# Half-channel slots for a selective scan, with scan input in matmul memory and C products on GpSimd

## The reference

```python
x = layernorm(x)                       # per position, over 256 features
x_ssm, z = split(x @ in_proj_w.T)      # 2 x 512 channels
xc = silu(causal_conv4(x_ssm) + conv_b)
xp = xc @ x_proj_w.T                   # 1 + 16 + 16 rows: dt_r, B, C
dt = softplus(dt_r @ dt_proj_w.T + dt_proj_b)
h  = exp(dt * A_n) * h + dt * B_n * xc # for each of 16 states n, over 512 positions
y  = sum_n(h_n * C_n) + xc * D
out = (y * silu(z)) @ out_proj_w.T
x1 = x + layernorm(out);  x2 = layernorm(x1)   # x2 feeds the attention block
scores = sigmoid(x2 @ w_sel)
```

## Time and profile before

| | us |
|---|---|
| median of three runs | 4357.64 |
| the profiled execution | 4360.78 |
| its span | 4358.8 |
| VectorE busy | 3630.8 (83%) |
| TensorE busy | 3803.9 (87%) |
| GpSimd busy | 2849.6 (65%) |
| ScalarE busy | 2029.6 (47%) |

### The profile page before, as it was taken

One profiled execution on the slowest core, in us unless ns is written; L12 is line 12 of the kernel. 1 busy time (PEld: TensorE's weight loads), 2 busy tenths in 40 slices (PEclk: granted clock), 3 DMA queues, 4 the chain that ended last, 5 costly groups with the idle time before them and its releaser, 6 DMA issues. The chain is left out here.

```text
span 4358.8 us, 54031 instructions
## 1 busy us (share of the span) xinstructions
PE 3803.9 (87%) x15744; PEld 2541.1 (58%) x15744; DVE 3630.8 (83%) x4012; ACT 2029.6 (47%) x3761; POOL 2849.6 (65%) x2524
## 2 busy tenths in 40 slices
PE   6777867867765599999999999999999999999787
PEld 2233323323322377777777777777777777777676
DVE  5999999999998478877887887887888788778598
ACT  4544535535443244544444444444444444444433
POOL 2758668567594366766766766766766766766444
PEclk8877877877876799999999999999999999999898
DMA  1000000000000300100100100100100100000101
GB/s 39 0 10 15 24 5 19 24 5 19 15 5 20 131 13 12 41 14 10 41 14 10 41 14 10 41 14 10 41 14 10 41 14 10 20 14 15 31 29 44
DMA packets 48726, 97.83 MB, mean 22 GB/s; under 512 B 3570, under 2 KB 33138, under 8 KB 46228
## 3 DMA queue, kind: packets, MB, share of 16 engines
q1 hardware_dynamic: 47620, 92.94, 6.2%
q0 software_dynamic: 1040, 4.19, 0.2%
HBM read 80.34 MB, written 16.78 MB: 22 GB/s over the span
## 5 line engine op out<-in xcount | busy, mean ns | idle before, releaser
L702 DVE TENSOR_TENSOR_SCAN state<-dA,dBx 128x2048 f32<-128x2048 f32 x128 | 726.8, 5678 | 25.9 <-POOL y_part L289 21.3
L1234 ACT ACTIVATE prob<-ps_b,negmax 128x512 f32<-128x512 f32 x512 | 346.1, 687 | 652.3 <-DVE negmax L1353 652.3
L286 POOL TENSOR_TENSOR state<-state,c_copy 128x1024 f32<-128x1024 f32 x120 | 345.5, 2879 | 374.8 <-DVE state L702 374.8
L1347 DVE TENSOR_TENSOR vg<-ps_b,gates 128x1024 f32<-128x1024 f32 x256 | 313.5, 1224 | 253.1 <-PE ps_b L1072 241.1
L961 POOL TENSOR_TENSOR qk_full<-vg 128x512 f32<-128x512 f32 x256 | 329.0, 1285 | 253.3 <-DVE vg L1347 253.3
L549 ACT ACTIVATE dA<-dt,a_neg 128x511 f32<-128x511 f32 x512 | 326.9, 711 | 323.9 <-DVE state L702 323.7
L974 POOL TENSOR_TENSOR ogT_low<-prob,ogT_high 128x512 fp32r<-128x512 f32 x256 | 324.0, 1295 | 208.9 <-ACT ogT_high L1267 208.9
L372 PE MATMUL ps_a<-xp_high,ident_r 33*128 33x512 f32 x256 | 163.0, 637 | 332.6 <-DVE dBx L692 307.9
L1070 PE MATMUL ps_b<-ogT_high,wo_high 128*128 128x512 f32 x1024 | 413.2, 403 | 11.1 <-DVE ogT_low L1399 10.8
L1070 PE MATMUL ps_b<-wv_high,xT_high 128*128 128x512 f32 x1024 | 414.6, 405 | 0.0
L289 POOL TENSOR_TENSOR y_part<-y_part,state 128x1024 f32<-128x1024 f32 x120 | 403.4, 3362 | 9.4
(11 more groups left out here) (237 smaller groups left out, 9530.9 us busy)
## 6 DMA issues: line engine op xcount, KB each, us to landing
xT<-xT_scratch SPq DMA_DIRECT2D x65, 512.0 KB, 3.3
wv<-in_wv SPq DMA_DIRECT2D x8, 1024.0 KB, 4.9
wo<-in_wo SPq DMA_DIRECT2D x8, 1024.0 KB, 7.0
x_in<-in_x SPq DMA_DIRECT2D x8, 512.0 KB, 4.7
x_a<-in_x SPq DMA_DIRECT2D x8, 512.0 KB, 5.3
x_scratch<-x_a SPq DMA_DIRECT2D x8, 512.0 KB, 2.9
xT_scratch<-x2T SPq DMA_DIRECT2D x8, 512.0 KB, 2.6
scores_scratch<-sg SPq DMA_DIRECT2D x8, 512.0 KB, 3.5
```

The lines of the kernel that those rows point to most:

```text
L286: pool.tensor_tensor(state, state, c, ALU.mult).then_inc(hc_part_done, 1)
L702: dve.tensor_tensor_scan(h[n % 2][:, :, :].rearrange("p c s -> p (c s)"), dA[n % 2][:, :, :].rearrange("p c s -> p (c s)"), dBx[n % 2][:, ...
L1234: act.activation(prob[h][:, t, :], ps[:, score_bank(t) + h, :], ACT.Exp, bias=negmax[:, t, h:h + 1], accum_out=total[:, h, t:t + 1]).then_ ...
```

## The change

1. *Half-channel slots.* A turn has 32 slots instead of 16 steps: slots 0 to 15 run all states over the first two channel blocks, 16 to 31 over the other two. `dA` and `h` become rings of four half-size buffers.
2. *`dBx` in PSUM.* It has no SBUF buffer any more, but two PSUM banks, one buffer in all. So the B product of slot s+1 waits for the scan of slot s, and the scan of s+1 for the product. B's spread gets two banks.
3. *C products on GpSimd.* GpSimd multiplies the whole half state by C_n, in place (L371 of the new kernel); TensorE sums all blocks. VectorE's C product, GpSimd's accumulation, `y_part`, ScalarE's copy and TensorE's spread of C go. C's 16 rows go to DRAM once a turn, and come back spread over all partitions in four DMAs of four rows (1 MB each).
4. *One product a spread.* The high and low parts of `xp` lie in one tile of 97 rows (`xp_parts`), and `pick` adds both in one product.
5. *Norms.* Combining and refining move to GpSimd (`combine_pool`, `newton_pool`), with one operation more a norm; statistics and normalising stay on VectorE.
6. *Order.* z is projected at the start of its own turn (slots 0 to 3) instead of at the end of the turn before; step sizes come in halves; `sum_y` runs two slots late; skip and gate come in halves (slots 2 and 18); scores are made in slots 30 and 31 instead of steps 8 to 10.

Cut to its core:

```diff
+        HALF = CB // 2
+        SLOTS = 2 * NS
+        RING, GROUP = 4, 4
+        Y_BANK, DBX_BANK, B_BANK = 0, 2, 4
-        dA, dBx, h = ([sb(f"{name}{n}", [P, CB, S]) for n in range(2)] for name in ("dA", "dBx", "state"))
+        dA, h = ([sb(f"{name}{n}", [P, HALF, S]) for n in range(RING)] for name in ("dA", "state"))
+        c_rows = sb("c_rows", [P, NS, S])
...
+            def load_c(b, q, weighed=None):
+                at = slice(q * GROUP, (q + 1) * GROUP)
+                rows = d["c_rows"][bass.ds(b, 1), at].rearrange("b n s -> b (n s)").partition_broadcast(P)
+                if weighed is not None:
+                    sp.wait_ge(hc_done, weighed)
+                sp.dma_start(c_rows[:, at, :].rearrange("p n s -> p (n s)").unsqueeze(1), rows).then_inc(c_loaded[q], 16)
...
             def turn(i, par, has_tail, has_head):
+                b, c = i + 1, i - 1
                 if has_head:
                     sp.wait_ge(ln_x.out_done, i * TT + TT)
-                    load_x(i + 1)
+                    load_x(b)
                 if has_tail:
-                    tail(i - 1)
+                    load_c(i, 3, i * SLOTS)
+                    residual(c)
+                if has_head:
+                    store_c(b)
+                    for q in range(3):
+                        load_c(b, q, i * SLOTS + NS + GROUP * (q + 1))
+                if has_tail:
+                    store_x2T(c)
+                    store_scores(c)
...
+            def weigh(i, s):
+                n, state = s % NS, h[s % RING][:, :, :]
+                pool.wait_ge(scan_done, i * SLOTS + s + 1)
+                if s < NS and n % GROUP == 0:
+                    pool.wait_ge(c_loaded[n // GROUP], i * 16 + 16)
+                pool.tensor_tensor(state, state, c_rows[:, n, :].unsqueeze(1).to_broadcast([P, HALF, S]), ALU.mult).then_inc(hc_done, 1)
...
+            def spread_b(b, s, par, first=False):
+                row = 1 + s % NS
+                if s == 0:
+                    pe.wait_ge(xp_low_done, b + 1)
+                if not first:
+                    pe.wait_ge(dBx_done, b * SLOTS + s - 1)
+                pe.matmul(ps[:, B_BANK + s % 2, :], pick[:, row:row + 1].to_broadcast([XPP, P]), xp_parts[par][:, :],
+                          start=True, stop=True).then_inc(b_psum, 1)
...
+            def inputs(b, s, par, first=False):
+                f = s // NS
+                if s % NS == 0:
+                    dve.wait_ge(du_done, b * CH + f + 1)
+                if not first:
+                    dve.wait_ge(scan_done, b * SLOTS + s)
+                dve.wait_ge(b_psum, b * SLOTS + s + 1)
+                dve.tensor_tensor(ps[:, DBX_BANK:DBX_BANK + HALF, :], half(du[par], f),
+                                  ps[:, B_BANK + s % 2, :].unsqueeze(1).to_broadcast([P, HALF, S]), ALU.mult).then_inc(dBx_done, 1)
+            def scan(i, s, first):
+                dve.wait_ge(dA_done, (i * SLOTS + s + 1) * HALF)
+                dve.wait_ge(dBx_done, i * SLOTS + s + 1)
+                if not (first and s < RING):
+                    dve.wait_ge(y_psum, i * SLOTS + s - RING + 1)
+                dve.tensor_tensor_scan(h[s % RING][:, :, :].rearrange("p c s -> p (c s)"),
+                                       dA[s % RING][:, :, :].rearrange("p c s -> p (c s)"),
+                                       ps[:, DBX_BANK:DBX_BANK + HALF, :].rearrange("p c s -> p (c s)"),
+                                       0.0, ALU.mult, ALU.add).then_inc(scan_done, 1)
```

The new `turn` of TensorE, which fixes what stands between the sums:

```diff
+                for s in range(SLOTS):
+                    if s + 2 < SLOTS:
+                        spread_b(i, s + 2, par)
+                    elif has_head:
+                        spread_b(b, s + 2 - SLOTS, 1 - par)
+                    if s < CB:
+                        project_z(i, s, has_tail)
                     if has_head:
+                        if s == 6:
+                            turn_input(b)
+                        elif 11 <= s < 15:
+                            project_x(b, s - 11, has_tail)
+                        elif 15 <= s < 23:
+                            convolve(b, (s - 15) // 2, range(0, 2) if s % 2 == 1 else range(2, 4))
+                        elif s in (24, 25):
+                            project_xp(b, 1 - par, range(2 * (s - 24), 2 * (s - 23)))
+                        elif s in (27, 28):
+                            project_dt(b, 2 * s - 54)
+                            project_dt(b, 2 * s - 53)
                     if has_tail:
+                        if 7 <= s < 11:
+                            project_out(c, s - 7, b if has_head else None)
+                        elif s == 29:
+                            turn_x2(c, b if has_head else None)
+                        elif s in (30, 31):
+                            select(c, s - 30)
+                    if s >= 2:
+                        sum_y(i, s - 2, has_tail or s - 2 >= NS)
+                    elif has_tail:
+                        sum_y(c, SLOTS - 2 + s, True)
```

More of the change, by code:

```diff
@@ L252, in _ @@
                 sp.dma_start(t[:], d[n]).then_inc(consts_loaded, 16)
+            store_c(0)
+            for q in range(NS // GROUP):
+                load_c(0, q)
             turns(sp, turn)
-            tail(NB - 1)
+            residual(NB - 1)
+            store_x2T(NB - 1)
+            store_scores(NB - 1)
             sp.wait_ge(x1_stored, CREDIT + 16 * NB)
@@ L291, in turn @@
[L291 to L302 removed]
+                low = xp_parts[par][LOW_ROW:XPP, :]
@@ new lines, in project_out @@
+            def project_out(c, t, b=None):
+                bank, at = EVEN[t // 2], slice(t * P, (t + 1) * P)
+                if t == 0:
+                    pe.wait_ge(yz_done, c * CH + CH)
+                    pe.wait_ge(zs_done, (c + 2) * CB if b is not None else NB * CB)
+                    if b is not None:
+                        pe.wait_ge(xnT_done, b * KD + KD)
+                for k in range(CB):
+                    mm = pe.matmul(ps[:, bank, (t % 2) * D:(t % 2 + 1) * D], yz[:, k, at], w_out[:, k, :],
+                                   start=(k == 0), stop=(k == CB - 1))
+                if t % 2:
+                    mm.then_inc(mo_psum, 1)
@@ L781, in _ @@
             last = NB - 1
-            skip(last, last % 2)
+            skip(last, 1, last % 2, first=True)
             stats_m(last)
```

612 lines of the change are left out of this document (306 added, 306 removed).

## The result

The changed kernel takes 4069.4 us, the median of four runs (4064.8 to 4070.1), against 4358.9 for the kernel before on the same chip (4356.7 to 4361.2, four runs): a ratio of 0.9335 (95% interval 0.9322 to 0.9348), 289 us less. The forecast was 4100, with a range of 4040 to 4215. The profiled execution took 4069.7 us with a span of 4067.9 and a mean granted clock of 0.972.

What follows compares the result with a forecast made beforehand. VectorE was taken to pace the first stage's loop: steady turns 171.0 to 138 us, six saving 198, first 30, last 28, rest 0, so 4360.8 becomes 4105, and the median, 3 lower, 4100 rounded; range 4040 to 4215.

Steps and rivals of the forecast that it cites:

- The step that carried the sum: On VectorE, with one input in matmul memory the scan stops taking turns with GpSimd and takes 2.29 us.
- Rival C: The scan still takes turns with GpSimd though one input left SBUF: slot 4.75, turn 164, 4305 us; 8%.
- 32 slots: VectorE's half states in a turn, each scan 2.29, B product 1.21, hand-overs 0.16: 3.66 us, 117 in all.
- other VectorE work: Rest of VectorE's turn: three times statistics and normalising, the residual add, four skip products: 12.3 us.
- stalls: VectorE waiting for late TensorE sums or the next input's load: 8.5 us a turn (ends 0 and 17).
- Rival D's cheap hand-overs: On VectorE, hand-overs as cheap as independent starts: slot 3.36 us, with the forecast's stalls 4023 us; 4%.
- the rival of dearer operands: Operands in matmul memory cost more than their rows say: each 0.1 us on an operation 51 us, 4150; 2%.
- each stretch at the lower level adds 1.7: TensorE, some 4.5 us late after slot 31, falls 1.7 us further behind with each stretch at the lower clock.
- The inventory of 117 us a turn: TensorE's work at the full level: 32 slots 69 us, projections and the rest 48, total 117, 12 under VectorE.
- Rivals B and E: B: TensorE becomes the bound at today's clock, 4240 us, 15%; E: TensorE stays at the lower level, above 4800 us, 5%.
- The ends: First turn 126 us, 30 less; last 130, 28 less; before and behind the loop 0, within 8 us either way.
- rival D's "no stall": Less is lost in the loop's turns: no stall, 4035 us; 9%.

Runs made afterwards that it cites:

- e1: The changed kernel with dBx in one SBUF buffer instead of two PSUM banks, order and waits the same: 4356.7 us, ratio 1.0002.
- e8: The kernel before with GpSimd's C product and accumulation for states 1 to 15 cut to the first of 512 positions: 4150.0 us, ratio 0.9525.
- e11: e1 with GpSimd's C product cut to the first of 512 positions: 4073.1 us, ratio 0.9348.
- e12: e11 with two SBUF buffers for dBx, so the B product waits only for the scan before the last: 4023.2 us, ratio 0.9233.
- e6: The changed kernel with VectorE's statistics and normalising operations laid singly into the gaps before and behind a B product: 4084.2 us.
- e4: The changed kernel with B's spread product done twice (4067.5 us) or four times (4085.2 us) in each slot.
- e9: The changed kernel with each normalising group between scan and B product, and GpSimd's C product of that slot held until the group is through: 4051.1 us.

## Why the prediction was right, and where its sizes were off

The step that carried the sum was that the scan stops taking turns with GpSimd once one input leaves SBUF. It holds: 2284 ns on average for 2.29 forecast, and e1, e8 and e11 show it from three sides. Rival C is out. e1 is what it describes, and shows it priced too low: 4305 forecast, 4357 measured, though the slot is 4.59 and not 4.75, since the waits of the other work were not in its price. The terms of one steady turn, by the starts of the fourth turn's scans:

| term | forecast | measured |
|---|---|---|
| 32 slots | 117 (3.66) | 119.4 (3.73) |
| other VectorE work | 12.3 | 13.4 |
| stalls | 8.5 | 2.3 |
| turn | 138 | 135.1 |

- *The slot.* Scan and GpSimd product were right to 0.01. The B product takes 1.23, not 1.21, and the hand-overs 0.12 and 0.09, not twice 0.08: 0.07 a slot, 18 us over the 256. Rival D's cheap hand-overs did not come, and neither did the rival of dearer operands: into matmul memory the B product takes 1229 ns, into SBUF 1221 (e11). The Trainium skill, "VectorE: DVE Perf Modes", section "The DRAIN you can't avoid", finds that a semaphore behind each of eight copies adds nothing over one behind the last. e12 is another test: it keeps every semaphore, lets the B product wait for the scan before the last instead of the one just ahead, and gets 0.24 us a slot. So what costs here is the wait, and no run tests the page's own case.
- *The other work.* Normalising was put at 1.4 us a norm and costs 2.03 of slot time (slot 5: 5.76 against 3.73), 1.9 more a turn. This is where the mechanism was incomplete. I had looked at operations with two SBUF tensors only; this one reads one, and still takes turns. The first stage before could not show it: none of its 96 normalising operations (405 to 414 ns) lay beside a GpSimd operation. The last stage of the same trace did, in the one that normalises from SBUF beside GpSimd:

```profile
L112 DVE TENSOR_SCALAR fn<-f,ln_avgb,ln_rstdb x32: 401/1340/1471, 4138.3 to 4344.9; 128x256 f32<-128x256 f32 x32
```

  The Trainium skill states it: "SBUF — State Buffer", section "Who interferes with whom", says that `tensor_scalar` can enter a two-port mode and then contends with GpSimd like an operation with two SBUF inputs, and that the other side blocks for the whole instruction. The rows agree: up to 1412 ns in the changed kernel, 2425 in e6. The statistics go the other way: a group of 1.41 adds only 1.13 to its slot, since it overlaps the B product ahead and the scan behind it.
- *The stalls.* This term was mis-sized most: 8.5 us a turn forecast, 2.3 measured. The next input's load was to be 2 to 6 us late a turn; VectorE waited for it 0.5 us in the whole loop. TensorE was to be 4.5 late behind slot 31; what VectorE waited for in the loop was this (us in total, times, longest):

```profile
DVE state L790 <- PE ps_a L503: 7.9, 15, 1.3
DVE ps_a L781 <- DVE state L790: 4.1, 12, 0.5
DVE state L790 <- issue: 4.1, 2, 2.0
```

  Seven turns share 7.9 us of waits for TensorE, in 15 scans. Twelve of these are the scans of slots 20 and 21, the other three those of slots 1, 4 and 5; the forecast had them at 30 to 3. Most begin with TensorE's order: in slot 18 it waits for the skip product, which stands behind VectorE's longest slot (17, 8.56 us):

```profile
532.84 3.78 PE L503 MATMUL ps_a<-state,ident 128*128 128x512 f32 x4 [7.65 <-DVE yz L802]
...
536.76 2.29 DVE L790 TENSOR_TENSOR_SCAN state<-dA,ps_a 128x1024 f32<-128x1024 f32 x1 [0.42 <-PE ps_a L503]
...
541.61 2.29 DVE L790 TENSOR_TENSOR_SCAN state<-dA,ps_a 128x1024 f32<-128x1024 f32 x1 [1.20 <-PE ps_a L503]
```

  After that wait the four products take 3.78 us, as at the lower level; the granted clock from 530 to 540 us is 0.55, and 0.93 in the 10 us ahead:

```profile
520.00:530.00 10.00, 5.19 (x13) 2.00 (x11) 9.71 (x12) 1.33 (x2) 3.94 (x9) 0.93 0.15 52
530.00:540.00 10.00, 7.16 (x10) 3.23 (x11) 9.19 (x8) 7.81 (x12) 8.87 (x9) 0.55 0.00 0
```

  The two waits that follow cost VectorE 1.6 us (0.42 and 1.20). They fit the forecast's "each stretch at the lower level adds 1.7", since four products at the full level take 1.9 us less; no run separates the clock from the late start.
- *TensorE.* The inventory of 117 us a turn came out at 116.9, and the loop's granted clock at 0.95, where 0.9 or more was named for the forecast. The close match is partly luck: 117 was counted at the full level, and this turn had a granted clock of 0.94, so at the full level its work is somewhat less. e4 shows the room left. Rivals B and E are out.
- *GpSimd and the C rows.* GpSimd is busy 95.5 us a turn, 105 forecast. The C rows load in 5.5 us each (4 to 5 forecast); in the loop nothing on VectorE or GpSimd is put down to them:

```profile
c_rows<-c_scratch SPq DMA_DIRECT2D x32, 1024.0 KB, 5.5
```

- *The ends.* First turn 121.1 (126 forecast), last 125.9 (130), the piece behind the loop within 2 us of before, as taken. The start is 4 us shorter (56.9 against 61.1), within the 8 allowed for. The stages behind are 5.5 us shorter, though nothing of theirs was changed. The cause stays open; the four runs of the kernel before alone lie up to 4.5 us apart.

The deviations are 2.4 + 1.1 - 6.2 = -2.7 us a turn, 17 us over six turns as the starts show them (215 less for 198 forecast), 9 in the first and last turn and 8 outside the loop: 34 of the 35 us between the sum of 4105 and the profiled execution's 4069.7. The measured time lies between the forecast and rival D's "no stall" (4035; its own sum, 4100 - 8 x 8.5, gives 4032): an error of the stalls partly balanced by one of the slot.

What stays open: how the gain splits over single edits is known for the norms (40) and the scan input (287). They overlap and don't add. Halving the slots, the order of z and the merged spread were not tried alone.

## What to carry to other kernels

Look at the spread of an instruction's durations before its mean: equal shapes with one fixed and one stretched time point to a shared resource, and the ends of the other engine's instructions show which. Where two engines take turns, taking other work off one of them earns nothing as long as the work that they take turns over stays the same in sum (e1). Here, moving one operand of the scan out of the shared memory did earn, and a short VectorE group was best kept together with the other engine held back for its length (e9). A wait of a VectorE operation for the one just ahead cost 0.2 us each time here, so independent work belongs between them.
